# Slot table built by whole groups, and up weights fetched slot by slot, in a one-core transformer kernel

## The reference

```python
# layer 1 ("gated"): softmax over 8 gates, top 2, renormalised
out = sum_e combine[:, e] * ((silu(x @ gate_e.T) * (x @ up_e.T)) @ down_e.T)
# layer 2 ("shared"): top 2 of 8, softmax over the two, and an expert that every token takes
shared = silu(x @ shared_w1.T) @ shared_w2.T
out = shared + sum_e gates[:, e] * (silu(x @ w1_e.T) @ w2_e.T)      # hidden width 512
```

## Time and profile before

| what | value |
|---|---|
| median of 3 timed runs | 3520.39 us (3518.59 to 3526.02) |
| profiled execution, its own time | 3524.75 us |
| its span in the profile | 3522.9 us |
| PE busy | 3013.2 us (86%) |
| DVE busy | 2406.2 us (68%) |
| ACT busy | 2049.6 us (58%) |
| POOL busy | 1153.8 us (33%) |
| DMA moved | 155.00 MB |

### The profile page before, as it was taken

One profiled execution on the slowest core, in us unless ns is written; L12 is line 12 of the kernel. 1 busy time (PEld: TensorE's weight loads), 2 busy tenths in 40 slices (PEclk: granted clock), 3 DMA queues, 4 the chain that ended last, 5 costly groups with the idle time before them and its releaser, 6 DMA issues. The chain is left out here.

```text
span 3522.9 us, 62960 instructions
## 1 busy us (share of the span) xinstructions
PE 3013.2 (86%) x21353; PEld 1948.5 (55%) x21353; DVE 2406.2 (68%) x6525; ACT 2049.6 (58%) x3059; POOL 1153.8 (33%) x1213
## 2 busy tenths in 40 slices
PE   4669999787758967999999869879778968997999
PEld 3533333344547962222222359859756956886787
DVE  7778888476876558999999475573286335656565
ACT  4459989664532335999999723344344435654565
POOL 4442311121547742001000077557636750001000
PEclk9879999998778988999999979989989989999999
DMA  1041210000011123001000121221202121001000
GB/s 59 1 132 59 70 50 22 1 1 25 1 72 34 49 75 108 21 21 30 21 21 12 44 105 49 67 96 53 73 21 69 52 87 66 1 1 39 31 10 13
DMA packets 80308, 155.00 MB, mean 44 GB/s; under 512 B 21872, under 2 KB 40112, under 8 KB 77696
## 3 DMA queue, kind: packets, MB, share of 16 engines
q1 hardware_dynamic: 59184, 105.08, 9.1%
q0 software_dynamic: 20816, 45.91, 4.5%
HBM read 102.09 MB, written 48.23 MB: 43 GB/s over the span
## 5 line engine op out<-in xcount | busy, mean ns | idle before, releaser
L2590 ACT ACTIVATE core_pr<-core_two 128x1024 f32<-128x1024 f32 (+3 forms) x896 | 787.5, 934 | 47.5 <-PE core_two L2557 43.8
L2626 DVE TENSOR_REDUCE core_mx<-core_one 128x1 f32<-128x512 f32 x778 | 491.4, 684 | 20.4 <-PE core_one L2509 13.0
L2569 PE MATMUL core_ps_o<-core_pr,core_vals 128*32 128x512 f32 (+3 forms) x3584 | 433.9, 559 | 1.7 <-ACT core_oT L2601 1.5
L2509 PE MATMUL core_one<-arena,queries 64*128 64x512 bf16 (+3 forms) x1472 | 374.6, 363 | 29.0 <-PEq L62 19.7
L2557 PE MATMUL core_two<-queries,arena 64*128 64x512 bf16 (+3 forms) x1792 | 340.8, 360 | 9.5 <-ACT core_pr L2590 6.8
L2509 PEld LDWEIGHTS core_one<-arena,queries 64*128 64x128 bf16 x1472 | 113.2, 94 | 296.0 <-DVE core_mx L2626 132.2
L2443 POOL COPY core_vals<-arena 128x288 f32<-128x288 f32 x32 | 14.7, 460 | 782.4 <-PE core_ps_o L2569 782.4
L2620 DVE CUSTOM_DVE_ANT_0 core_junk<-core_one,core_over 128x512 bf16<-128x512 f32 (+4 forms) x334 | 201.7, 644 | 26.6 <-PE core_one L2509 21.9
L585 PE MATMUL moe_first_bank<-moe_first_xrT,moe_first_chosen_w 128*128 128x128 f32 x1704 | 217.0, 278 | 2.3 <-DVE moe_first_xrT L830 2.2
L585 PE MATMUL moe_second_bank<-moe_second_xrT,moe_second_chosen_w 128*128 128x128 f32 x1704 | 215.5, 277 | 2.0 <-DVE moe_second_xrT L830 1.9
L585 PEld LDWEIGHTS moe_first_bank<-moe_first_xrT,moe_first_chosen_w 128*128 128x128 f32 x1704 | 204.6, 194 | 4.4 <-DVE moe_first_xrT L830 4.2
(11 more groups left out here) (637 smaller groups left out, 7170.2 us busy)
## 6 DMA issues: line engine op xcount, KB each, us to landing
arena<-expert_out SPq DMA_DIRECT2D x64, 256.0 KB, 3.7
expert_rows<-arena SPq DMA_DIRECT2D x13, 512.0 KB, 3.0
q_parts<-qkv_parts SPq DMA_DIRECT2D x16, 384.0 KB, 2.6
k_parts<-qkv_parts SPq DMA_DIRECT2D x16, 384.0 KB, 3.5
queries<-q_parts SPq DMA_DIRECT2D x64, 96.0 KB
arena<-k_parts SPq DMA_DIRECT2D x64, 96.0 KB
moe_first_w_up<-in_m_up SPq DMA_DIRECT2D x3, 2048.0 KB, 8.6
moe_second_w_up<-in_m_up SPq DMA_DIRECT2D x3, 2048.0 KB, 9.7
```

The lines of the kernel that those rows point to most:

```text
L2509: pe.matmul(one[bank[e]][:, 0:width], q_sb[rows, hq, pair, qt * P:(qt + 1) * P], k_sb[rows, hq, pair, kc * CW:kc * CW + width], start=True ...
L2569: mm = pe.matmul(ps_o[h * 32:(h + 1) * 32, off:CW], vals[:, hq % 2, j, h, :], pr[:, (n * N2 + k) % KEPT, h // 2, h % 2, off:CW], start=(j ...
L2590: a.activation(pr[:, step % KEPT, i, :, off:CW], two[spot[e] % 2][:, :, off:CW], ACT.Exp, scale=HD ** -0.5).then_inc(s_wide, 1)
L2626: v.tensor_reduce(at, scores, AX.X, ALU.max).then_inc(s_read, 1)
```

## The change

The table: DVE compares a whole group at once (`hits`, eight tiles by 71 slots), makes `lanes` for k = 0 to 4 in one operation, and multiplies `hits` by the tile numbers for the first half of `cells`. POOL keeps k = 5, 6, 7 (`ALONE`). The second half of `cells` moves to ACT, as an activation with the token number as scale, at the head of each round of its program; PE's product waits for it too (`s_tokens`). This holds for all four stages.

The shared stages: `w_up`, its load and `choose_w` go. Instead SP, once `woff` is there, loads each slot's offset into a register and fetches 256 KB of that expert's up weights from DRAM into one of eight buffers of `chosen_w`, waiting before slot s for the up product of slot s - 8. PE's `up(s)` waits for that fetch. `EVERY` is 4, so the last unit is at slot 68, and `ADDED` is moved to match. The gated stages keep `w_up` and DVE's copy.

```diff
-    w_up = st.sb("w_up", [P, halves * W])
+    w_up = st.sb("w_up", [P, halves * W]) if gated else None
-    HT = 4
+    HT, WB = 4, 2 if gated else 8
+    hits = st.sb("hits", [P, 2, GT, SLOTS], BF16)
-    chosen = st.sb("chosen_w", [P, 2, halves, HID])
+    chosen = st.sb("chosen_w", [P, WB, halves, HID])
+    s_fetched = [st.sem(f"w_fetched{i}") for i in range(8 if shared else 0)]
-    s_aside = st.sem("lanes_aside")
-    OTHERS = (1, 3, 5, 7)
+    s_aside, s_tokens = st.sem("lanes_aside"), st.sem("tokens")
+    ALONE = range(5, GT)
-    AT, EVERY = 4, 3
+    AT, EVERY = 4, 4
-    ADDED = {7: 3, 19: 4, 31: 5, 43: 6, 52: 7}
+    ADDED = {9: 3, 25: 4, 41: 5, 57: 6, 69: 7}
...
# SP
-            for f in range(halves):
+            for f in range(halves if gated else 0):
...
+            if shared:
+                sp.wait_ge(s_chain, WOFF)
+                for s in range(SLOTS):
+                    e = sp.value_load(woff[0:1, s:s + 1], min_val=0, max_val=7 * HID)
+                    if s >= WB:
+                        sp.wait_ge(s_up, s - WB + 1)
+                    sp.dma_start(chosen[:, s % WB, 0], up_all[:, 0:W][:, bass.ds(e, HID)]).then_inc(s_fetched[s % WB], 16)
# POOL
-                for k in OTHERS:
+                for k in ALONE:
# PE
                 pe.wait_ge(s_cells, n + 1)
+                pe.wait_ge(s_tokens, n + 1)
...
-                pe.wait_ge(s_wc, s + 1)
+                if gated:
+                    pe.wait_ge(s_wc, s + 1)
+                else:
+                    pe.wait_ge(s_fetched[s % WB], 16 * (s // WB + 1))
# ACT
-            if shared:
-                for n in range(GROUPS_T * TOPK):
-                    if n in TURNED_AT:
-                        copy_xn(4 + TURNED_AT.index(n))
-                    if n + 1 < GROUPS_T * TOPK:
-                        always(ASIDE)
-                    if n < GT // 2:
-                        normalise(3, range(2 * n, 2 * n + 2))
+            for n in range(GROUPS_T * TOPK):
+                if n >= 2:
+                    a.wait_ge(s_table, n - 1)
+                a.wait_ge(s_first, n + 1)
+                a.activation(cells[:, n % 2, :, SLOTS:2 * SLOTS], hits[:, n % 2], ACT.Identity, scale=r.token).then_inc(s_tokens, 1)
+                if shared and n in TURNED_AT:
+                    copy_xn(4 + TURNED_AT.index(n))
+                if n + 1 < GROUPS_T * TOPK:
+                    always(ASIDE)
+                if shared and n < GT // 2:
+                    normalise(3, range(2 * n, 2 * n + 2))
# DVE
-                for k in range(GT):
-                    j = n * GT + k
-                    if k not in OTHERS:
-                        v.tensor_scalar(lanes[:, n % 2, k, :], r.laneb[:], lo[:, j:j + 1], None, ALU.is_equal)
-                    last = v.tensor_scalar(cells[:, n % 2, k, 0:SLOTS], r.slotb[:], hi[:, j:j + 1], float(j + 1), ALU.is_equal, ALU.mult)
-                last.then_inc(s_first, 1)
+                group_n = slice(n * GT, (n + 1) * GT)
+                few = slice(n * GT, n * GT + ALONE[0])
+                v.tensor_tensor(hits[:, n % 2], r.slotb[:].unsqueeze(1).to_broadcast([P, GT, SLOTS]),
+                                hi[:, group_n].unsqueeze(2).to_broadcast([P, GT, SLOTS]), ALU.is_equal).then_inc(s_first, 1)
+                v.tensor_tensor(lanes[:, n % 2, 0:ALONE[0]], r.laneb[:].unsqueeze(1).to_broadcast([P, ALONE[0], P]),
+                                lo[:, few].unsqueeze(2).to_broadcast([P, ALONE[0], P]), ALU.is_equal)
                 v.wait_ge(s_first, n + 1)
-                v.tensor_scalar(cells[:, n % 2, :, SLOTS:2 * SLOTS], cells[:, n % 2, :, 0:SLOTS], 0.0, r.token, ALU.is_gt, ALU.mult).then_inc(s_cells, 1)
+                v.tensor_tensor(cells[:, n % 2, :, 0:SLOTS], hits[:, n % 2], r.slotb[:, n * GT + 1:(n + 1) * GT + 1].unsqueeze(2)
+                                .to_broadcast([P, GT, SLOTS]), ALU.mult).then_inc(s_cells, 1)
...
             v.wait_ge(s_chain, WOFF)
-            v.wait_ge(s_wl, 16 * halves)
-            choose_w(0)
+            if gated:
+                v.wait_ge(s_wl, 16 * halves)
+                choose_w(0)
```

More of the change, by code:

```diff
@@ L584, in up @@
                     for j in range(4):
-                        mm = pe.matmul(out[s % 2][:, j * P:(j + 1) * P], chosen[:, s % 2, half, j * P:(j + 1) * P],
+                        mm = pe.matmul(out[s % 2][:, j * P:(j + 1) * P], chosen[:, s % WB, half, j * P:(j + 1) * P],
                                        xrT[:, s % 2, :], start=True, stop=True)
@@ L598, in _ @@
             pe.wait_ge(s_chain, WOFF)
-            pe.wait_ge(s_wl, 16 * halves)
+            if gated:
+                pe.wait_ge(s_wl, 16 * halves)
             turn_x(0)
@@ L816, in _ @@
                 add(2)
-            w_by_half = w_up[:].rearrange("p (f n) -> p f n", f=halves)
+            w_by_half = w_up and w_up[:].rearrange("p (f n) -> p f n", f=halves)
             def choose_w(s):
@@ L844, in _ @@
                 if s + 1 < SLOTS:
-                    choose_w(s + 1)
+                    if gated:
+                        choose_w(s + 1)
                     copy_x(s + 1)
```

## The result

The changed kernel took 3558.50 us (median of 5 runs, 3549.47 to 3562.46) beside 3520.39 (3518.59 to 3526.02) for the kernel before: ratio 1.0094, 95% interval 1.0074 to 1.0115. The forecast was 3525.2 with a range of 3513 to 3537. It was wrong: the time lies outside the range, and nearly 1% is well past the 0.2% that I called the limit. The profiled execution is the shortest of the five: 3549.47 with a span of 3547.6, 24.7 over the span of 3522.9.

A forecast was written before the change was run, and what follows sets the result against it. Limits taken: POOL's columns (gated table), POOL, DVE and PE nearly full (shared table), POOL's transfers (shared slot loop). -8.0 + 12.6 + 0.2 = +4.8 us made the profiled 3524.75 into 3529.5; the median, 4.4 below, 3525.2; range 3513 to 3537.

The forecast's parts named there:

- I add 0.04 for disturbing each other: 8 x 2.13 = 17.0: Gated table: DVE and POOL tie near 2.0 us a round; 17.0 against 21.0, -4.0 a stage, -8.0 together.
- POOL is held up by the new DVE operations: Rival, gated tables: at 0.827 us a column the gain shrinks to 1.2 a stage, sum +10.4, 3530.8 us; chance 14%.
- the rule: From the GPSIMD reference: GpSimd's SBUF interface suffers from VectorE instructions in a two-port mode or with two SBUF inputs.
- hold POOL the whole round: Table: DVE's new operations, all with two SBUF inputs, would block POOL throughout; priced only at 0.827 us a column.
- The ring over ScalarE: Shared tables: PE's next table waits for ACT's tokens behind the silu; rounds 25.27 us against 19.27, +12.6 over two stages.
- The shared tables: Both shared stages' tables grow by 6.1 and 6.5 us, including 0.1 and 0.25 for ACT's copies before the first tokens.
- The slot loops: Shared stages: transfers -1.5, first weights +1.2, unit spacing -0.5, last unit +0.9; +0.1 a stage, +0.2 together.
- that rival: Shared tables: PE's idle holes lower its clock; at half clock +21 us over 14 rounds, 3546 us; chance 8%.
- The prices of the new operations: Table: DVE's 568 columns at 0.67 us start to start, 2.09 a round for three operations; ACT's tokens 0.75.

The follow-up runs named there:

- both_second: The changed kernel run once more, unchanged, on another chip: 3554.26 us, ratio 1.0089 to the kernel before.
- lanes_single: The kernel before with the new table alone, DVE's five lanes columns made one by one on one tensor and a scalar: 3538.72 us, ratio 1.0043.
- tokens_early: The changed kernel with ACT making the next round's tokens before its copy, silu and normalisation: 3700.11 us, ratio 1.0068, where the kernel before takes 3674.72.
- dve_early: The kernel before with the new table alone, all lanes columns on DVE and the next round's tokens ahead of ACT's shared work: 3519.91 us, ratio 0.9987.
- weights_second: The kernel before with only SP's weight fetches, eight buffers and units on every fourth slot, measured a second time: 3526.96 us, ratio 1.0005.
- again: The changed kernel run once more, unchanged, on the chip where the kernel before takes 3674.72 us: 3714.92 us, ratio 1.0106.
- table_second: The kernel before with the new table alone, measured a second time: 3551.01 us, ratio 1.0076.

## Why the prediction was wrong

- *The step that failed* is the gated table, "I add 0.04 for disturbing each other: 8 x 2.13 = 17.0". It took the price of POOL's column from beside other DVE operations, 0.657 us. Beside the new ones it is 1.03 on average (24.78 / 24), and 1.40 to 1.51 while DVE works without a pause (1.82 in the first column). -8.0 forecast, +7.6 measured: 15.6 us too low. Had this term been right, the sum for the profiled execution would have been 3545.1 of the 3549.5.
- *What no term accounts for.* The median of 3558.5 is 33.3 us above the forecast, and the profile explains 19.9 of them (15.6 here, most of the rest in the shared tables). The other 13.4 come from how the profiled executions lie to their medians: 4.4 above it before, 9.0 below it after. The two shorter executions had a mean granted clock of 0.933 and the three longer ones 0.927 to 0.930, but none of the three was profiled, and `both_second` stood only 30 us over the kernel before. This part stays open.
- *The rival had the cause, not the size.* "POOL is held up by the new DVE operations" was there with 14%, priced at the longest of the 32 old columns, 0.827. That row was measured beside operations on one tensor, so it was no bound for the ones on two. I had the rule and gave it a chance but no price of its own; "hold POOL the whole round" should have been worked out: if a column lasts as long as the DVE operations that it overlaps, two of 0.75 give 1.5, and three columns more than a round of DVE. The Trainium skill (SBUF — State Buffer, section "Who interferes with whom") goes further than the page that I used: a VectorE instruction with two SBUF inputs contends with a GpSimd instruction that reads SBUF, for ports that the section calls an exclusive lock. The traces agree that such operations disturb GpSimd strongly (0.60 to 1.51) and one-tensor ones much less (`lanes_single`, mean 0.86); GpSimd still got one column for two VectorE operations. They don't settle that it is a full block and not a slowing: in the shared table, a column that starts 0.40 us before the burst ends takes 0.85 us, where 0.40 of waiting and 0.60 of work would be 1.00.
- *The ring over ScalarE* was right, and in this profile right in size: 25.70 us of rounds against 25.27. It was the largest term. `tokens_early` and `dve_early` show it by taking it away.
- *The shared tables* were +8.4 and +8.8 instead of +6.1 and +6.5. The missing 2 us are the first product, for which I had allowed 0.1 and 0.25 of ScalarE's copies: POOL's first three columns meet DVE's first burst and take 1.82, 1.40 and 1.51 us, as in the gated tables, and silus stand ahead of the tokens. In the changed kernel the two end within half a microsecond; with no POOL columns the start is at 4.8 and 3.3 us instead of 5.1 and 5.1.
- *The slot loops* were right at about nothing (+0.2 forecast, -0.3 and +0.3 in the profile), and on the chip of `weights_second` the part takes 1.0005. That its cost hangs on the chip was not foreseen.
- *The clock* stayed at 1.00 in the shared tables of the first profile, but not in those of `again`, `both_second` and `table_second` (0.90 to 0.95), where the shared tables took 1.3 to 1.7 us more. So that rival was right that the clock can fall beside a hole, and wrong in which one and in size: it fell in the wait for the first product, not in the holes of the ring, and that cost about 3 us in all instead of 21.
- *The prices of the new operations* were near: 568 columns 0.74 to 0.75 alone and 0.74 to 0.88 beside POOL (0.67 from start to start), tokens on ACT 0.75 to 0.77 as worked out.

## What to carry to other kernels

Before turning many small VectorE operations on one tensor into few large ones on two, look at what GpSimd does beside them: here fewer and larger operations made VectorE 1.8 us quicker in a gated table (20.0 to 18.2) and GpSimd's share 3.8 slower (21.0 to 24.8), and the table ends with the slower. Take GpSimd out, or leave it one piece a round. And when an operation moves to an engine that is only half busy, draw that engine's program order around it: what counts is what stands ahead of it and waits, not how much time is free; here moving it ahead of the round's shared work was worth 11 us on two tables.

## What the runs showed of the hardware

- A GpSimd `tensor_scalar` of 128 columns in bf16 takes 0.60 us beside an idle VectorE and 0.61 to 0.73 beside its `tensor_scalar` operations (one of 32: 0.83). Beside back-to-back `tensor_tensor` operations of 0.74 to 0.9 us it takes 1.40 to 1.51 (the first of a table 1.82), one column to two operations; where the burst ends during the column, 0.85. The mean over a table is 1.03 with three columns a round, 1.33 with two, and 1.55 with one (12.4 us for 8): the fewer columns, the larger the part of them that meets VectorE at work, so such a mean can't be carried from one split to another.
- VectorE is little disturbed in return: 568 columns take 0.74 to 0.75 us with GpSimd idle, 0.79 on average beside it. Eight columns of lanes at once (1024 wide) take 1.22 with GpSimd idle; seven take 1.09, six 0.98 and five 0.86 beside it.
- The kernel before takes 3520 to 3526 us in four sets of executions and 3675 on another chip. In the shared slot loops of that chip TensorE has idle times of up to 3.6 us that nothing in the profile accounts for, with 256 KB a slot of weights fetched beside it or without (elsewhere 0.7 in the kernel before and 1.3 in `table_second`).
- After 3.40 us without a matmul in the shared table of `both_second`, TensorE's granted clock fell from 2.4 to 1.2 GHz for 3.4 us as the next product began; the round took 5.1 us instead of 3.8.
